# Computing the attention's R in two halves, placed behind the bias passes of the duo two before it

## The reference, cut to what matters

```
qk   = x @ W_qk.T + b_qk                 # 4 heads x 64 query columns, and 32 key columns
q, k = split(qk)                         # both cut into 16 x 16 windows of 64 pixels
attn = einsum('bxyhcp,bxyhdp->bxyhcd', q, k) * temperature   # per window and head: 64 x 8
out  = attn, laid out again as an 8 x 8 window of pixels, 4 heads x 8 channels
```

## Time and profile before

| What | us |
|---|---|
| runs of the kernel before | 852.43, 854.88 (median), 855.67 |
| the profiled execution | 860.17 |
| its span, from the first to the last instruction | 858.2 |
| TensorE matmuls busy | 667.5 (78%) |
| ScalarE busy | 553.8 (65%) |
| VectorE busy | 542.8 (63%) |

### The profile page before, as it was taken

One profiled execution on the slowest core, in us unless ns is written; L12 is line 12 of the kernel. 1 busy time (PEld: TensorE's weight loads), 2 busy tenths in 40 slices (PEclk: granted clock), 3 DMA queues, 4 the chain that ended last, 5 costly groups with the idle time before them and its releaser, 6 DMA issues. The chain is left out here.

```text
span 858.2 us, 22838 instructions
## 1 busy us (share of the span) xinstructions
PE 667.5 (78%) x9588; PEld 433.1 (50%) x9588; DVE 542.8 (63%) x1165; ACT 553.8 (65%) x572; POOL 240.7 (28%) x285
## 2 busy tenths in 40 slices
PE   5477777599878889699888769968879888547774
PEld 4322222199856656545411159955656486115553
DVE  4647767579944534346589979964434545967670
ACT  4899999554355558699889754435557700927774
POOL 4511111185045510000000048124530000038771
PEclk9879999989989999799999989989999989658887
DMA  9432221000000000000000000000000000004667
GB/s 313 155 88 83 79 75 51 1 2 2 1 2 4 4 3 2 1 2 2 26 2 2 1 2 2 2 1 4 4 3 2 2 26 1 0 1 147 196 205 236
DMA packets 59908, 37.15 MB, mean 43 GB/s; under 512 B 1952, under 2 KB 59424, under 8 KB 59808
## 3 DMA queue, kind: packets, MB, share of 16 engines
q1 hardware_dynamic: 59808, 35.71, 13.7%
HBM read 18.93 MB, written 16.78 MB: 42 GB/s over the span
## 5 line engine op out<-in xcount | busy, mean ns | idle before, releaser
L741 ACT ACTIVATE work<-X,l0s 128x2048 f32<-128x2048 f32 (+2 forms) x80 | 138.4, 1760 | 5.0 <-POOLq L311 5.0
L756 ACT ACTIVATE work<-ps 128x2048 f32<-128x2048 f32 x64 | 120.9, 1890 | 22.7 <-PE ps L444 22.1
L444 PE MATMUL ps<-work,cst 32*32 32x512 f32 x2048 | 76.3, 623 | 36.2 <-ACT work L756 25.2
L528 PE MATMUL ps<-cst,work 128*128 128x143 f32 x640 | 93.1, 290 | 0.0
L776 ACT ACTIVATE work<-ps 128x512 f32<-128x512 f32 x80 | 47.9, 599 | 60.4 <-PE ps L517 60.4
L528 PEld LDWEIGHTS ps<-cst,work 128*128 128x128 f32 x640 | 84.3, 194 | 0.5 <-ACT work L776 0.5
L1250 POOL TENSOR_TENSOR co<-mv,cst 128x1 f32<-128x1 f32 x7 | 1.3, 190 | 293.3 <-DVE mv L877 200.4
L976 DVE TENSOR_TENSOR X<-X,ps 128x512 f32<-128x512 f32 x64 | 43.7, 683 | 61.0 <-PE ps L457 61.0
L457 PE MATMUL ps<-work,w2d 128*32 128x512 f32 x512 | 70.5, 618 | 2.2 <-ACT work L756 2.2
L794 ACT ACTIVATE work<-ps 128x520 f32<-128x520 f32 x64 | 38.7, 604 | 48.2 <-PE ps L576 47.9
L1351 POOL TENSOR_TENSOR work<-X,work 128x1024 f32<-128x1024 f32 (+1 forms) x32 | 60.5, 1918 | 25.7 <-ACT work L845 25.6
(11 more groups left out here) (140 smaller groups left out, 1240.2 us busy)
## 6 DMA issues: line engine op xcount, KB each, us to landing
out<-work SPq DMA_DIRECT2D x64, 256.0 KB, 3.2
work<-x SPq DMA_DIRECT2D x16, 512.0 KB, 5.3
work<-x SPq DMA_DIRECT2D x32, 256.0 KB, 2.8
work<-choose SPq DMA_DIRECT2D x8, 128.0 KB, 2.7
cst<-consts SPq DMA_DIRECT2D x1, 1009.5 KB, 9.2
cst<-consts SPq DMA_DIRECT2D x1, 64.0 KB, 1.9
```

Of the source, the lines that this page charges most:

```text
L444: last = pe.matmul(ps[C * m:C * m + C, g, :], wg[rows, m, C * g:C * g + C], y_piece(i, j, m)[rows, :], start=True, stop=True)
L528: last = pe.matmul(ps[:, DEEP + 2 * (q % 2) + par, at:at + OW * OH], patch[:, q, k, :], c("fir"), start=True, stop=True)
L741: act.activation(o, x_in.rearrange("p (j n) -> p j n", n=BANK), ACT.Gelu, scale=l0s[:, at:at + 1], bias=l0s[:, at + MULTI:at + MULTI + 1]) ...
L756: act.activation(zb[:, k % ZDEEP, :, :], ps[:, 0:4, :], ACT.Gelu).then_inc(s_zs, 1)
```

## The change: what it does

`r_sum` gets a second argument and does one half: half 1 the 16 matmuls of j = 2 and 3 (array rows 64 to 127, banks 2 and 3), half 0 those of j = 0 and 1 (rows 0 to 63, banks 0 and 1). Each half gives one count on s_r, so ScalarE can copy a half by itself; it copies half 1 first and half 0 second. Ahead of the loop both R of duo 0 and R of duo 1 are made, each as half 1 and then half 0. In the loop, r_back(i) issues the half r_sum(i+2, 1) behind pair 0's biases and r_sum(i+2, 0) behind pair 1's biases; before, r_sum(i+1) stood whole ahead of r_back(i). The half waits (L617) for the copy of the same half of duo i+1. The order of ScalarE's list stays as it was, copies of duo i and then squares of duo i-1.

```diff
-                def r_sum(i):
+                def r_sum(i, half):
...
                     if nn:
-                        pe.wait_ge(s_rc, 2 * nn)
+                        pe.wait_ge(s_rc, 2 * nn - half)
                     for hd in range(HEADS):
                         for hp in range(2):
-                            for j in range(4):
+                            for j in range(2 * half, 2 * half + 2):
...
                     for pair in range(2):
-                        pe.wait_ge(s_rc, 2 * nn + pair + 1)
+                        pe.wait_ge(s_rc, 2 * nn + 2 - pair)
...
                                       start=False, stop=True).then_inc(s_xt, 1)
+                        if i + 2 < DUOS:
+                            r_sum(i + 2, 1 - pair)
...
-                r_sum(0)
+                for half in (1, 0):
+                    r_sum(0, half)
                 project_m(DUOS - 1)
-                r_sum(1)
+                for half in (1, 0):
+                    r_sum(1, half)
                 turn_keys(1)
                 for i in range(DUOS):
-                    if i and i + 1 < DUOS:
-                        r_sum(i + 1)
                     r_back(i)
...
-                    act.wait_ge(s_r, nn + 1)
...
-                    for j in range(0, 4, 2):
+                    for k, j in enumerate((2, 0)):
+                        act.wait_ge(s_r, 2 * nn + 1 + k)
                         act.activation(rs[:, i % RING, 4 * j:4 * j + 8, :]...
```

## The result

The changed kernel takes 882.51 us (median of 4 runs, 879.80 to 883.31), the kernel before 855.27 beside it (4 runs, 852.43 to 862.08): ratio 1.027 with a 95% interval of 1.021 to 1.033, so 18 to 28 us slower. I had forecast slower, 874.7, which is a ratio of 1.023. The direction and the mechanism came out; the median lies 7.8 us above the forecast and just outside the range that I gave (882.0), while the ratio's interval holds the forecast.

A forecast was written before the change was run, and what follows sets the result against it. TensorE bounds the kernel at 5.30 us a duo; 0.87 + 1.10 + 7.95 - 0.04 = 9.88 a set, 19.8 for two, on the median 854.88 gives 874.7 us. Range 863 to 882.

The forecast's parts named there:

- The loop: Biases, adds, square, copy, hand-over, half, turns: 6.89 us a duo against 5.30, five times, 7.95 a set.
- No overlap: In r_back, a half behind a pair's biases doesn't run beside them, so it gains nothing of its 1.10 us.
- my first rival: Halves run beside the biases while the 6.89 us period stays: 8.1 us a set, 871.2 in all; chance 0.22.
- The half: One half of r_sum alone on TensorE costs 1.10 us, with 0.57 and 1.14 as ends.
- The count of records: Rival: a half of r_sum costs 0.57 us, as its 32 records decide; 865.5 in all; chance 0.08.
- The ends: Outside the five periods of each set: r_sum(0) +0.87 us, r_sum(1) hidden, r_back(0) +1.10, after duo 5 -0.04.
- the end: From duo 5's biases to the last: whole r_sum(7) of 1.14 us goes, a half of 1.10 stays, -0.04.
- that fall as a rival in the loop: TensorE's new idle time lowers its clock, costing 1.59 us more a duo, 16 over ten: 891; chance 0.05.

The follow-up runs named there:

- the whole start: Changed kernel with r_sum(0) and r_sum(1) made whole again as in the kernel before, loop as changed: 879.35 us, ratio 1.022.
- after_again: The changed kernel measured once more, unedited: 886.68 us, ratio 1.033.
- after_third: The changed kernel measured yet again, unedited: 882.76 us.
- both edits: Changed kernel with ScalarE's copies ahead of squares and each bias matmul split into two of 64 columns: 858.66 us, ratio 1.003.
- the halving alone: Kernel before with each r_sum issued as half 1 then half 0, in the old place with the old waits: 868.15 us, ratio 1.012.
- before_again: The kernel before measured once more, unedited: 852.68 us.

## Why the prediction was right, and where its sizes were off

**The loop: right.** The step on which it rested was that half 1 is asked for (at 4.24) before the copy, behind the squares, lets it go (4.77). The trace has that wait five times a set, the period is 6.85 for the forecast 6.89, and putting the copies ahead removes it. Five periods at 1.55 are 7.75 a set, for 7.95.

**No overlap: right, and for the reason weighed.** The half starts 1.06 after the biases. Giving the biases the shape of the passes, as two matmuls of 64 columns for one of 128, lets it start after 0.03, with nothing else changed. The Trainium skill's page TensorEngine Tiling (Array Packing), section Tiling Modes, says that a change of mode drains TensorE; 1.06 against 0.03 agrees with it. What I left out is what running beside would be worth: my first rival priced it as free, and it costs 0.46 a half (1.52 for 1.06). It didn't matter for the forecast, but it is why the best version with halves stays at 5.08 a duo.

**The half: near.** I took 1.10 between 0.57 and 1.14; it takes 1.03 to the next weight load, near what eight records on one tile need if they follow each other. The count of records would have given 0.57.

**The ends.** Two halves of r_sum(0) take 1.58 before project_m(7) starts in the third profile's second set (648.60 to 650.18), for 1.16 in the first set before (302.56 to 303.72): +0.42, for my +0.87, which added two halves as if only a little of them overlapped. r_back(0) +1.03 for 1.10, the end -0.10 for -0.04 (9.35 for 9.45). Together 0.42 + 1.03 + 7.75 - 0.10 = 9.1 a set, 18.2 in all, where I had 19.8.

**What the sum left out.** The part grew on average from 46.41 (four sets of two profiles) to 56.93 (six sets of three), 10.5 a set, 21.0 in all. The 2.8 between 18.2 and 21.0 fit the clock, and some idle time, at the beginning of the part: with the fall a set took 57.66, without it 55.57 in the same execution, although 1.0 us of the 55.57 is idle time inside project_m(7) that the other set doesn't have (told of at the end). It fell in four of these six sets and in one of the four before. Two sets have neither the fall nor that idle time, the first of the kernel before (45.51) and the first of the whole start (54.19). They are 8.7 apart, 9.1 with the 0.42 of the halved start, so this much is the loop and the ends alone. I had that fall as a rival in the loop, at 0.05; it came at the start instead, where I gave it 0.5 in the range only. The rest, up to the 27.2 between the medians, lies outside the change: the output step at the end takes 99.7 us from its first to its last spread in one execution of the kernel before and 106.8 in the other, and 106.7 to 108.1 in the changed kernel's three. That is the clock again, 0.97 against 0.85 over most of this stretch (the second execution's, then the first's; columns as in the earlier trace rows):

```profile
773.00:828.00 55.00, 38.20 (x292) 25.75 (x288) 41.91 (x61) 45.72 (x36) 48.77 (x25) 0.97 0.67 200
```

```profile
773.00:835.00 62.00, 45.23 (x298) 33.03 (x295) 44.88 (x61) 47.17 (x37) 47.54 (x25) 0.85 0.61 183
```

The chain that ended last shows where it costs, here at one of its groups: 16 turns of the output on TensorE take 1.98 us in the second execution and 3.58 in the first, where the clock granted over them is 1.00 and 0.53 (start, us, what; the second execution's, then the first's):

```profile
797.26 1.98 PE ps L707 x16
798.75 3.58 PE ps L707 x16
```

Of the 7.5 us between the two executions (860.17 and 852.68) this step makes 7.1. The kernel before has runs from 851.84 to 867.60; that its other runs differ for the same reason is likely but not shown, as only two were traced. The changed kernel's repeats lie 24.6 (after_again) and 20.6 (after_third) above the medians of the kernel before beside them, so 27.2 is partly the draw; 21 is what the traces show of the change. Why the changed kernel's profiles all had the longer output step is not settled. It doesn't go with the slower loop: with both edits, at 5.08 a duo, the step takes 107.5 too, and with the halving alone 99.7.

## What to carry to other kernels

Before work is issued earlier, follow the buffer that it overwrites to the instruction that frees it, and that one to its place in its own engine's order: here the passes came two microseconds sooner and the copy that frees their bank stood behind two squares that wait for the very biases in between. Free rows of the array were not enough to run beside a neighbour here; the two needed the same tile shape, and even then price the pair, not the longer of the two. And where run-to-run spread is 10 us, compare the stretch that changed, by its own landmarks in the trace.

## What the runs showed that I had not expected

- Splitting a 128-column bias into two matmuls of 64 columns costs nothing by itself: pair alone 1.02 us to the next weight load, for 1.06.
- Two halves on different rows, one behind the other, take 1.55 us, one alone 1.03, the whole 1.14, and a half beside a pair of biases adds 0.46 to 0.48, by the order.
- In some executions TensorE sits idle for 0.65 to 1.02 us in the middle of project_m(7) of the second set, released by nothing that the profile shows, in the kernel before (before_again) as in the changed one (here after, second set). It is in neither sum:

```profile
649.93 0.38 PE L607 MATMUL ps<-work,cst 32*32 32x256 f32 x1 [1.02 <-issue]
```
